# Changing the sizes of the last groups of node bins in a graph and expert layer

## The reference

```python
xn  = layernorm(x)
agg = segment_sum(xn[dst], src, num_segments=6250)   # gathers 100000 rows
x   = x + ((agg + xn) @ W1 + b1) @ W2 + b2
y   = layernorm(x)
w   = softmax(y @ Wr + br)
h   = relu(bn1(y @ eW1[e] + eb1[e]))                 # for each of 8 experts
h   = relu(bn2(h @ eW2[e] + eb2[e]))
x   = x + sum_e w[:, e] * (h @ eWo[e] + ebo[e])
```

## Time and profile before

| | |
|---|---|
| median of 3 timed runs | 1381.36 us (1381.16 to 1383.55) |
| profiled execution, its span | 1595.0 us |
| first gather, last gather issued | 235.8 us, 1497.0 us |
| first group's first matmul | 295.2 us |
| PE busy | 1279.8 us, 80% |
| DVE busy | 1197.4 us, 75% |
| ACT busy | 868.3 us, 54% |
| POOL busy | 805.0 us, 50% |

### The profile page before, as it was taken

The page is one execution under the profiler, slowest core; times in us unless marked ns, Lnnn a source line. Parts: engine busy times, 40 slices in busy tenths (PEclk is TensorE's granted clock), DMA queues, the critical chain, the costliest instruction groups (busy, mean ns, idle before and its releaser), DMA issues.

```text
span 1595.0 us, 25908 instructions
## 1 busy us (share of the span) xinstructions
PE 1279.8 (80%) x8179; PEld 841.9 (53%) x8179; DVE 1197.4 (75%) x3476; ACT 868.3 (54%) x1623; POOL 805.0 (50%) x864
## 2 busy tenths in 40 slices
PE   3868885557687778888878878898888998788998
PEld 3746652345454445455545545554555666565665
DVE  9999985566667666777777877777778887777865
ACT  7887451344455435454445544555545665555685
POOL 3000006666556666666666666666666556656300
PEclk9969997778799988999999999999999999999999
DMA  9301135333232332333333333343333323332200
GB/s 292 99 0 53 54 100 170 109 98 103 83 103 86 110 91 87 111 88 100 102 89 113 87 90 113 87 116 87 89 111 88 107 83 107 88 105 86 74 11 11
DMA packets 82235, 150.86 MB, mean 95 GB/s; under 512 B 16855, under 2 KB 55034, under 8 KB 82100
## 3 DMA queue, kind: packets, MB, share of 16 engines
q0 software_dynamic: 39840, 108.84, 23.8%
q1 hardware_dynamic: 42260, 40.36, 8.0%
HBM read 129.87 MB, written 19.27 MB: 94 GB/s over the span
## 4 chain that ended last, share of the span: by engine, by line
PE 47%; DVE 24%; issue 12%; another core or an unknown queue 8%; ACT 7%; DVEq 2%; ACTq 0%
PE PA L1555 11%; PE PB L1571 11%; DVE acc L1071 5%; PE PL L1589 4%; DVE zz L837 4%; PE PT L1589 4%; PE PN L1589 3%; DVE zz L838 3%; DVE onehot L1002 2%; DVE xt L1190 2%; ACT PB L742 2%; PE PN L1505 2%; PE PT L1505 1%; PE PT L1504 1%
## 5 line engine op out<-in xcount | busy, mean ns | idle before, releaser
L544 POOL DMA_INDIRECT gbuf<-xn_hilo,dsti x830 | 790.3, 952 | 667.5 <-issue 196.8
L741 ACT ACTIVATE h<-PB,bnt,bns 128x512 f16<-128x512 f32 (+3 forms) x240 | 167.7, 699 | 325.9 <-remote 177.5
L1555 PE MATMUL PA<-yT,wsplit 128*128 128x512 f16 (+3 forms) x1440 | 318.1, 361 | 13.0 <-issue 9.4
L1571 PE MATMUL PB<-h,wsplit 128*128 128x512 f16 (+3 forms) x1440 | 300.3, 347 | 5.6 <-issue 5.6
L730 ACT ACTIVATE h<-PA,bnt,bns 128x512 f16<-128x512 f32 (+3 forms) x240 | 167.8, 699 | 215.8 <-remote 104.2
L1555 PEld LDWEIGHTS PA<-yT,wsplit 128*128 128x128 f16 x1440 | 143.3, 103 | 114.9 <-issue 31.3
L1173 DVE TENSOR_TENSOR h<-PB,h 128x512 f16<-128x512 f32 (+3 forms) x240 | 139.9, 587 | 84.8 <-ACT PB L742 64.5
L1571 PEld LDWEIGHTS PB<-h,wsplit 128*128 128x128 f16 x1440 | 141.2, 101 | 98.3 <-issue 13.0
L1002 DVE TENSOR_SCALAR onehot<-iota_row,srel 128x128 f16<-128x128 f16 x830 | 178.2, 267 | 0.0
L1167 DVE TENSOR_TENSOR h<-PA,h 128x512 f16<-128x512 f32 (+3 forms) x240 | 139.5, 587 | 40.2 <-ACT PA L731 31.8
L1071 DVE TENSOR_TENSOR acc<-acc,PN 128x256 f32 x276 | 114.0, 413 | 71.9 <-issue 23.8
(11 more groups left out here) (250 smaller groups left out, 1856.5 us busy)
## 6 DMA issues: line engine op xcount, KB each, us to landing
gbuf<-xn_hilo,dsti POOLq DMA_INDIRECT x830
xt<-x_whole_bins SPq DMA_DIRECT2D x49, 128.0 KB
out<-xt SPq DMA_DIRECT2D x49, 128.0 KB
acc<-in_x SPq DMA_DIRECT2D x4, 1536.0 KB
x_whole_bins<-acc SPq DMA_DIRECT2D x4, 1536.0 KB, 11.8
xn_hilo<-xt SPq DMA_DIRECT2D x24, 256.0 KB, 2.1
h<-in_L_ffn_W SPq DMA_DIRECT2D x9, 256.0 KB, 4.3
zz<-in_L_ffn_W SPq DMA_DIRECT2D x5, 256.0 KB
```

The costliest lines, as they stand in the source:

```text
L544: pool.indirect_dma_start(gbuf[:, k % SLOTS, :], None, xn_dram, bass.IndirectOffsetOnAxis(dsti[:, k:k + 1], 0)).then_inc(gat[k % SLOTS], 16)
L741: nc.scalar.activation(h2[:, e % 2, 0, h, 0:w], PB[:, h, 0:w], ACT.Relu, bias=sh, scale=sc)
L1555: last = T_.matmul(PA[:, h, 0:w], wsp[0][:, e, k, wp, h * P:(h + 1) * P], yT[:, g % 2, yp, k, 0:w], start=n == 0, stop=n == 5)
L1571: last = T_.matmul(PB[:, h, 0:w], wsp[1][:, e, k, wp, h * P:(h + 1) * P], h1[:, e % 2, yp, k, 0:w], start=n == 0, stop=n == 5)
```

## The change

The list of sizes is another. Fifteen groups become seventeen: one group of four less, four groups of three at the end become three, and three groups of two and one of one follow.

```diff
@@ -46,7 +46,7 @@
 TILES = -(-E_EDGES // P)
 BOUND = TILES + BINS - 1
 GT = 4
-GS = [1, 2, 3, 3] + [GT] * 7 + [3] * 4
+GS = [1, 2, 3, 3] + [GT] * 6 + [3] * 3 + [2] * 3 + [1]
 G = len(GS)
 FIRST = [sum(GS[:g]) for g in range(G + 1)]
 NENT = BOUND
```

## The result

| | before | after |
|---|---|---|
| median of 4 timed runs each | 1381.91 us (1381.16 to 1383.55) | 1405.43 us (1404.85 to 1408.0) |
| ratio | | 1.0173, 95% interval [1.0161, 1.0185] |
| profiled execution, its span | 1379.6 us (taken again, below) | 1402.8 us |

The change costs 23.5 us (forecast 15.9: 1397, range 1373 to 1409). It is slower by 1.7%, as forecast, and inside the range; a third of the cost was not foreseen.

A forecast was written before the change was run, and what follows sets the result against it. The prediction took TensorE's own matmul time to bound the late groups, so only added idle counts. Its five terms summed to +15.9 us on the 1381.4 us median, giving 1397 us, range 1373 to 1409.

The forecast's parts named there:

- TensorE is late, not the gathers: Late part of the kernel: gathers run ahead and fill the ring, 24.7 us in 17 waits for one bank.
- 1, two-bin steps: Two-bin groups: L3 waits for L2's activations, 0.7 us idle a step, charged only in the third group: +3.3 us.
- 2, one-bin group: Last group: steps of 3.05 us against 1.95 of work, plus two waits at the end: +9.0 us.
- 3, two more seams: Two added group boundaries: TensorE waits for ScalarE's table loads and normalising, 3.5 us each: +7.0 us, bounds 0 and 12.
- 4, ninth group: Ninth group: 31 pairs for 34 save 7.5 us if gathers bound it; a third taken: -2.5 us.
- 5, output: End of the kernel: three stores issued over 1.38 us become one: -0.9 us.
- The clock: One-bin steps: idle halves TensorE's clock to 1.2 GHz, +1.0 us a step, +8: 1405 us; chance 0.13.
- Gathers bind to the last pair: Groups eleven to sixteen: gathers set the pace, so the shorter tail wins about 8 us: 1373 us; chance 0.15.
- Nothing measurable: Whole kernel: pairs and the ninth group's gain cover the added idle, change within 0.2%, 2.8 us; chance 0.08.

The follow-up runs named there:

- fourteen groups: The kernel before with group sizes 1 2 3 3 and ten fours, one group fewer: 1385.08 us, ratio 1.0019.
- without the table loads: Small early activations move ScalarE's table loads off the seams, in both kernels: before 1381.08 us, ratio 0.9994; changed 1402.48 us, ratio 1.0154.
- the run with other places: The changed kernel with one pair a step moved to place 0, two pairs to places 0 and 4: 1403.64 us, ratio 1.0157.

## Why the prediction was right, and where it was short

**The bound.** "Where TensorE is the bound, the shorter tail is paid for by the groups ahead of it, and only idle time counts": held for the late part. The reading that led there was partly wrong. "TensorE is late, not the gathers" failed for the kernel before: in the paused profile the ring looked full for long; in the undisturbed one the gathers go at 1.25 us each with hardly a wait, and the kernel before is held by gathers and TensorE about equally. The conclusion survived because both are near their limit in the ninth group and behind it; fourteen groups show the side that the prediction did not see.

**The sum.** Measured as idle time, against the terms:

| term | forecast | measured |
|---|---|---|
| 1, two-bin steps: waits ahead of L3 | +3.3 | +5.8 |
| 2, one-bin group, less the last three-bin group | +9.0 | +8.9 |
| 3, two more seams | +7.0 | +7.3 |
| 4, ninth group | -2.5 | +0.1 |
| 5, output | -0.9 | -1.1 |
| sum | +15.9 | +21.0 |

The spans differ by 23.2; the rest is the 2 us of the first eight groups told of above. The +7.3 of term 3 is a remainder: all idle time that is in no other term, the 1.7 us at the lower clock in before's last seam counted as idle. No run sets the two seams apart from the rest, and without the table loads the change still cost 21.4 us, so its nearness to 7.0 is partly luck. How the measured terms come about: I took each distance between two starts on TensorE beyond the usual one of its line as idle ahead of the second instruction. Ahead of L3 the three two-bin groups lose 1.7, 2.2 and 1.9 us: 5.8. The one-bin group has 14.6 - 5.7 = 8.9 more than the last group before, 11 of its 14.6 ahead of L3. The ninth group loses 4.1 for 4.0. All other idle is 20.5 - 5.8 = 14.7 in the two-bin groups and 15.6 - 4.1 = 11.5 in the wide ones, where it was 22.9 - 4.0 = 18.9 before: +7.3. In the three narrow seams themselves TensorE waits 6.1 + 4.7 = 10.8 us, 3.6 each for the 3.5 of the forecast.

**Two steps failed.** One is in term 1, mis-sized at 3.3 for 5.8 us: "In the first two two-bin groups two pairs a step (0.87 us) fill it: I cost them nothing". They lose 3.9 us ahead of L3. In the second of them, two L1 a step apart, and the L3 between:

```profile
1301.83 0.82 PE L1555 MATMUL PA<-yT,wsplit 128*128 128x256 f16 x6
...
1303.81 1.47 PE L1589 MATMUL PN<-wsplit,h 128*128 128x256 f16 x12
...
1306.86 0.82 PE L1555 MATMUL PA<-yT,wsplit 128*128 128x256 f16 x6
```

The step takes 5.03 us for 3.91 + 0.87 = 4.78 of work. In the first the wait ahead of L3 is from nothing up to this:

```profile
1257.01 1.47 PE L1589 MATMUL PT<-wsplit,h 128*128 128x256 f16 x12 [1.03 <-issue]
```

In the rows above, VectorE adds the pair of place 3 from 1302.97 on and subtracts the second half from 1303.30, though ScalarE had finished with it at 1302.85. The text had named the danger ("if they stand in the wrong place, 16 x 0.7 = 11 us") and kept it as a bound only. A step with one pair (third group) takes 4.81 us for 4.35 of work, so a pair closes only 0.25 of a gap of 0.7. One such step, from L3 to L3:

```profile
1347.50 1.47 PE L1589 MATMUL PT<-wsplit,h 128*128 128x256 f16 x12 [0.28 <-issue]
...
1349.90 0.82 PE L1571 MATMUL PB<-h,wsplit 128*128 128x256 f16 x6
...
1350.75 0.56 ACT L741 ACTIVATE h<-PB,bnt,bns 128x256 f16<-128x256 f32 x1
...
1351.78 0.42 DVE L1173 TENSOR_TENSOR h<-PB,h 128x256 f16<-128x256 f32 x1 [0.23 <-ACT PB L742]
...
1352.31 1.47 PE L1589 MATMUL PL<-wsplit,h 128*128 128x256 f16 x12 [0.28 <-issue]
```

Here VectorE is not late: it waits 0.23 us for ScalarE. The pair stands on TensorE between the two halves of L2, so the second half ends 0.44 us later, and ScalarE takes it up 1.09 us after the first (at 1349.66). With the pair between the halves of L1, in the run with other places, it does so after 0.91 us, and the step is shorter by the same 0.18 us, 4.62, that of a step without a pair. The third group, forecast at 3.3, lost 1.9 ahead of L3; in its seam step the one long wait at L1535 covers this gap too.

The other is term 4, "so I take a third: -2.5", measured at +0.1. Fewer pairs shortened the ninth group by 1.2 us (83.8 to 82.6), which is the 3 x 0.435 of their matmuls; the gathers' 3 x 2.5 gave nothing, as TensorE was within 4 us of full in both.

**One-bin steps** came as forecast. The steady steps of the last group:

```profile
1383.62 0.81 PE L1589 MATMUL PN<-wsplit,h 128*128 128x256 f16 x6 [0.94 <-ACT PB L742]
1384.27 0.83 PE L1571 MATMUL PB<-h,wsplit 128*128 128x128 f16 x12
...
1386.71 0.81 PE L1589 MATMUL PL<-wsplit,h 128*128 128x256 f16 x6 [0.94 <-ACT PB L742]
...
1395.99 0.82 PE L1589 MATMUL PL<-wsplit,h 128*128 128x256 f16 x6 [1.61 <-ACT PB L742]
```

3.09 us a step (forecast 3.05), and 1.61 at the end twice (forecast 1.75).

**The rivals.** *The clock*: its number, 1405, is the one that was measured, but not for its reason. After each of these waits 12 matmuls of 128 columns take 0.83 us as in the earlier trace rows, the page shows the full 9 to the end, and the granted clock is 1.00 in the last stretch, the higher of the two levels. The Trainium skill (TensorE: Matmul & The Clock Gate, HAM oscillation) has this for bursts between longer waits; in the one-bin steps, with waits of 0.94 and at the end 1.6 us, it does not come about here. The clock does fall elsewhere, in seams: in before's last one and in several of the experiments. It does not follow from the wait alone. These are L3's six matmuls in the last group, behind a wait of 1.64 us for the router's weights in both, after (granted 1.00) and with only the last group split (0.50 from 1366.6 to 1370.0 us):

```profile
1377.43 0.82 PE L1589 MATMUL PL<-wsplit,h 128*128 128x256 f16 x6
```

```profile
1366.79 1.49 PE L1589 MATMUL PL<-wsplit,h 128*128 128x256 f16 x6
```

*Gathers bind to the last pair*: in fourteen groups they do, after they don't. But it named half of the truth, that the kernel before is at that limit. *Nothing measurable*: false.

## What to carry to other kernels

Splitting the last groups to shorten the tail pays only where the engine that does the split-off work has time to do it sooner. Here the work is the same number of matmul columns, and each narrower step falls below the length of its own chain of ScalarE and VectorE (4.6 us for two bins, 3.1 for one, against 3.9 and 1.95 of matmuls); before splitting, compare the two per size, and stop at the size where the chain becomes longer. Filler work between the matmuls covers a gap only by what it doesn't itself add to the chain that the gap waits for, on whichever engine. And a queue that runs without a gap to its end, as the gathers do here, never recovers what it once had to wait.

## What was not expected of the hardware

- A profiled execution can be far from the timed ones: 1595.0 us against 1379.6 for the same kernel, with pauses in which all engines stop. Busy times grew too (PE 1279.8 against 1211.4 us), and waits changed their releasers. A profile whose span is well over the timed median should be taken again before rows of waits are read from it.
- In the one-bin steps eight activations with a row of 0.42 to 0.48 us each start 0.34 to 0.36 us apart, so ScalarE's steady pace there is 2.8 us of a 3.09 us step. Its busy time per row overstates what it takes in sequence; the forecast's 2.1 us for the way to L3 came from the rows and was still close.
- TensorE's clock fell to 0.50 in some seams and not in others with the same wait ahead (rows above), and it cost 1.7 us in one seam of before and up to 5.7 us in two seams of the run with other places. Differences of one to three us between two single profiles can come from it.
- Why the first eight groups end up to 4 us apart in the profiles was not looked into. Whether another split of VectorE's work could shorten the narrow seams was not tried either, nor another plan of pairs for the changed sizes, which could lay more of them into the thirteenth group, where gathers wait.
